# A new order of PE, ACT and DVE within the eight cycles of a batch of the first layer

## The reference

```
x = x + attn(layernorm(x))
  dist   = arccosh(1 + 2*|q-k|^2 / ((1-|q|^2)*(1-|k|^2)))
  out    = softmax(-dist) @ v ; out @ wo.T
x = x + moe(layernorm(x))
  logits = x @ router_w.T ; the 8 largest of 64 probabilities, normalised
  routed = sum over the 8 experts of weight * expert(x), at most 128 tokens each
  shared = (silu(x @ gate) * (x @ up)) @ ws_down
```

## Time and profile before

| | us |
|---|---|
| median of 3 runs (3197.37 to 3205.93) | 3198.28 |
| profiled execution, its own time | 3206.46 |
| its span | 3204.7 |
| PE, DVE, ACT, POOL busy | 2482.1, 2018.2, 1689.0, 1891.3 |
| mean granted clock of PE over the span | 0.84 |

### The profile page before, as it was taken

The page is one execution under the profiler, slowest core; times in us unless marked ns, Lnnn a source line. Parts: engine busy times, 40 slices in busy tenths (PEclk is TensorE's granted clock), DMA queues, the critical chain, the costliest instruction groups (busy, mean ns, idle before and its releaser), DMA issues. The chain is left out here.

```text
span 3204.7 us, 31378 instructions
## 1 busy us (share of the span) xinstructions
PE 2482.1 (77%) x10153; PEld 1156.9 (36%) x10153; DVE 2018.2 (63%) x3045; ACT 1689.0 (53%) x2384; POOL 1891.3 (59%) x1886
## 2 busy tenths in 40 slices
PE   4567677676766677665398699999999999999995
PEld 2222233232322222223155344444444444444442
DVE  4797868687887868672133366575656565656564
ACT  1677767767777677882022254544444444444351
POOL 0544566666756666784577304683847565655675
PEclk7667777777777787776699799999999999999996
DMA  2000000000000100002499600000000000000000
GB/s 93 14 1 1 15 14 14 15 14 15 7 9 14 15 14 7 16 9 27 113 280 263 148 1 1 1 1 20 1 20 1 21 1 14 7 7 1 7 1 14
DMA packets 95157, 99.12 MB, mean 31 GB/s; under 512 B 19825, under 2 KB 91761, under 8 KB 94961
## 3 DMA queue, kind: packets, MB, share of 16 engines
q1 hardware_dynamic: 70784, 74.12, 8.2%
q0 software_dynamic: 24176, 22.70, 3.9%
HBM read 74.30 MB, written 26.80 MB: 32 GB/s over the span
## 5 line engine op out<-in xcount | busy, mean ns | idle before, releaser
L849 POOL TENSOR_TENSOR TT<-TT,SS 128x512 f32<-128x512 f32 x512 | 651.7, 1307 | 407.9 <-ACT SS L780 407.6
L1540 ACT ACTIVATE PR<-S,NM 128x512 f32<-128x512 f32 x512 | 347.0, 683 | 579.9 <-DVE NM L1707 579.9
L1707 DVE TENSOR_REDUCE NM<-S 128x2 f32<-128x1024 f32 x256 | 313.1, 1223 | 289.1 <-PE S L1444 288.8
L372 PE MATMUL OB<-TT,VAL 128*17 128x512 f32 x1024 | 350.9, 790 | 87.0 <-ACT TT L788 86.8
L613 DVE TENSOR_SCALAR TT<-SC 128x1024 f32<-128x1024 f32 x256 | 311.5, 1217 | 132.9 <-PE SC L351 61.9
L854 POOL DMA_INDIRECT slot_tokens<-TID,IDX x256 | 258.1, 1008 | 116.4 <-issue 86.3
L615 DVE SCALAR_TENSOR_TENSOR SS<-SC,TT 128x1024 f32<-128x1024 f32 x256 | 313.6, 1225 | 20.6 <-issue 1.8
L1444 PE MATMUL S<-KT,QT 64*128 64x512 f32 x1024 | 308.2, 670 | 0.7 <-ACT QT L1509 0.7
L1473 PE MATMUL OT<-PT,VN 128*64 128x512 f32 x1024 | 284.6, 635 | 2.9 <-ACT PT L1546 2.1
L1455 PEld LDWEIGHTS TP<-ident,PR 128*128 128x128 f32 x2048 | 227.4, 141 | 147.2 <-issue 119.5
L1455 PE MATMUL TP<-ident,PR 128*128 128x128 f32 x2048 | 275.4, 278 | 5.4 <-DVE PT L1712 4.9
(11 more groups left out here) (258 smaller groups left out, 4317.4 us busy)
## 6 DMA issues: line engine op xcount, KB each, us to landing
WG<-w_gu SPq DMA_DIRECT2D x64, 384.0 KB
WD<-w_dn SPq DMA_DIRECT2D x64, 128.0 KB
stream<-rows SPq DMA_DIRECT2D x1, 4224.0 KB, 17.1
XL<-x SPq DMA_DIRECT2D x8, 512.0 KB, 4.3
X<-x SPq DMA_DIRECT2D x8, 512.0 KB, 4.0
rows<-XL SPq DMA_DIRECT2D x8, 512.0 KB
slot_tokens<-TID,IDX POOLq DMA_INDIRECT x256
stream<-X SPq DMA_DIRECT2D x8, 512.0 KB
```

The lines of the kernel that those rows point to most:

```text
L372: ins = pe.matmul(OB[r:r + DH0 + 1, :], values_of[:, mt, h, :], TT[:, h % RING, mt, :], start=(mt == 0), stop=(mt == NT - 1))
L849: ins = pool.tensor_tensor(tt[:, mt, :], tt[:, mt, :], ss[:, mt, :], ALU.add)
L1540: act.activation(PR[s % 2][h2][:], S[s % 2][:, h2, :], ACT.Exp, bias=NM[:, s % 2, h2:h2 + 1], accum_out=SM[:, pair % 2, j, h2:h2 + 1]).the ...
L1707: dve.tensor_reduce(NM[:, s % 2, :], S[s % 2][:], AX, ALU.max, negate=True).then_inc(sems["peak"], 1)
```

## The change

The lists are ordered anew, and three things move in the engines' own order:

- ACT: the first root stands ahead of slot 0. Slot 1 moves from between the roots to behind the second root and the table load, slot 2 from there to behind the first logarithm (with slot 3). `Silu` stays behind the second root.
- PE: the first score quarter of the next pair comes behind slot 3; the second comes behind the late tasks and slot 5, directly ahead of `query_norms`; slot 6 comes last.
- Tasks: `logits` from cycle 5 to 6, `weights` ahead of `slots`, `shared` 0 from cycle 1 to 0, `output` 1 and `stats2` from cycle 3 to 4, `turn_hid` 0 from cycle 0 to the end of the cycle 7 before it. Evictions go from slots 4 to 6 to others.

Numbers and kinds of operations stay as they are; one wait for `took_a` is added ahead of the first `gate_up`.

```diff
 TO_ACT = [
-    (0, 1, "turn_hid", 0, "before2"), (0, 2, "turn_hid", 1, "before2"),
-    (0, 4, "refill", 12, "this"), (0, 5, "refill", 13, "this"), (0, 6, "refill", 14, "this"), (1, 0, "refill", 15, "this"),
-    (1, 1, "turn", 0, "after"), (1, 2, "turn", 1, "after"),
-    (1, 4, "project", 0, "after"), (1, 5, "project", 1, "after"), (1, 6, "project", 2, "after"), (2, 0, "project", 3, "after"),
-    (3, 1, "turn_ao", 0, "before"), (3, 2, "turn_ao", 1, "before"),
-    (5, 0, "refill", 0, "after"), (5, 1, "turn2", 0, "before"), (5, 2, "turn2", 1, "before"),
-    (5, 3, "refill", 1, "after"), (5, 4, "refill", 2, "after"), (5, 5, "refill", 3, "after"),
-    (6, 0, "refill", 4, "after"), (6, 1, "refill", 5, "after"), (6, 3, "refill", 6, "after"), (6, 4, "refill", 7, "after"),
-    (7, 0, "refill", 8, "after"), (7, 1, "refill", 9, "after"), (7, 3, "refill", 10, "after"), (7, 4, "refill", 11, "after"),
+    (0, 1, "refill", 12, "this"), (0, 3, "turn_hid", 1, "before2"), (0, 6, "refill", 13, "this"),
+    (1, 0, "refill", 14, "this"), (1, 1, "turn", 0, "after"), (1, 2, "refill", 15, "this"),
+    (1, 2, "turn", 1, "after"), (1, 5, "project", 0, "after"), (1, 6, "project", 1, "after"),
+    (2, 0, "project", 2, "after"), (2, 1, "project", 3, "after"), (3, 0, "turn_ao", 0, "before"),
+    (3, 3, "turn_ao", 1, "before"), (5, 0, "refill", 0, "after"), (5, 0, "refill", 1, "after"),
+    (5, 0, "turn2", 0, "before"), (5, 1, "refill", 2, "after"), (5, 2, "turn2", 1, "before"),
+    (5, 5, "refill", 3, "after"), (6, 1, "refill", 4, "after"), (6, 2, "refill", 5, "after"),
+    (6, 3, "refill", 6, "after"), (6, 4, "refill", 7, "after"), (7, 1, "refill", 8, "after"),
+    (7, 3, "refill", 9, "after"), (7, 4, "refill", 10, "after"), (7, 4, "refill", 11, "after"),
+    (7, 5, "turn_hid", 0, "before"),
 ]
 TO_DVE = [
-    (0, "late", "stats", 0, "after"), (0, "late", "take_group", 2, "before"), (0, "late", "place_group", 2, "before"),
-    (0, "late", "norm", 0, "after"),
-    (1, "early", "shared", 0, "before2"), (1, "early", "shared", 1, "before2"),
-    (2, "late", "take_group", 3, "before"), (2, "late", "place_group", 3, "before"), (2, "late", "values", 0, "after"),
-    (2, "late", "norms", 0, "after"), (2, "late", "values", 1, "after"), (2, "late", "clamp_sign", 0, "after"),
-    (3, "early", "clamp_apply", 0, "after"), (3, "late", "output", 0, "before"), (3, "late", "output", 1, "before"),
-    (3, "late", "stats2", 0, "before"),
-    (4, "late", "take_group", 0, "this"), (4, "late", "split", 0, "after"), (4, "late", "split", 1, "after"),
-    (4, "late", "place_group", 0, "this"), (4, "late", "norm2", 0, "before"),
-    (5, "late", "split", 2, "after"), (5, "late", "logits", 0, "before"), (5, "late", "gate_up", 0, "before"),
-    (5, "late", "gate_up", 1, "before"), (5, "late", "split", 3, "after"),
-    (6, "early", "gate_up", 2, "before"), (6, "early", "gate_up", 3, "before"), (6, "late", "take_group", 1, "this"),
-    (6, "late", "split", 4, "after"), (6, "late", "split", 5, "after"), (6, "late", "place_group", 1, "this"),
-    (7, "early", "slots", 0, "before"), (7, "late", "split", 6, "after"), (7, "late", "split", 7, "after"),
-    (7, "late", "weights", 0, "before"),
+    (0, "early", "take_group", 2, "before"), (0, "late", "stats", 0, "after"), (0, "late", "shared", 0, "before2"),
+    (0, "late", "place_group", 2, "before"), (0, "late", "norm", 0, "after"), (1, "early", "shared", 1, "before2"),
+    (2, "late", "take_group", 3, "before"), (2, "late", "values", 0, "after"), (2, "late", "norms", 0, "after"),
+    (2, "late", "values", 1, "after"), (2, "late", "place_group", 3, "before"), (2, "late", "clamp_sign", 0, "after"),
+    (3, "early", "clamp_apply", 0, "after"), (3, "late", "output", 0, "before"), (4, "early", "output", 1, "before"),
+    (4, "early", "stats2", 0, "before"), (4, "late", "take_group", 0, "this"), (4, "late", "split", 0, "after"),
+    (4, "late", "place_group", 0, "this"), (4, "late", "norm2", 0, "before"), (4, "late", "split", 1, "after"),
+    (5, "early", "split", 2, "after"), (5, "late", "gate_up", 0, "before"), (5, "late", "gate_up", 1, "before"),
+    (5, "late", "split", 3, "after"), (6, "early", "logits", 0, "before"), (6, "early", "split", 4, "after"),
+    (6, "early", "take_group", 1, "this"), (6, "late", "gate_up", 2, "before"), (6, "late", "gate_up", 3, "before"),
+    (6, "late", "split", 5, "after"), (6, "late", "place_group", 1, "this"), (7, "early", "weights", 0, "before"),
+    (7, "early", "slots", 0, "before"), (7, "early", "split", 6, "after"), (7, "early", "split", 7, "after"),
 ]
...
             def gate_up(v, j, par):
+                if j == 0:
+                    turned_in(v)
                 product(item_d(v), j, wgu, 2 * F).then_inc(sems["work_d"], 1)
...
                 attend(v, par, p, 3, **of)
+                a_slot(v, a_parts, par, p, 3, **of)
                 if follows:
                     scores(v, ahead, 0)
-                a_slot(v, a_parts, par, p, 3, **of)
-                if follows:
-                    scores(v, ahead, 1)
                 a_slot(v, a_parts, par, p, 4, **of)
                 d_tasks(v, d_parts, par, p, ("late",), **of)
                 a_slot(v, a_parts, par, p, 5, **of)
-                a_slot(v, a_parts, par, p, 6, **of)
+                if follows:
+                    scores(v, ahead, 1)
                 if follows:
                     query_norms(v, ahead)
+                a_slot(v, a_parts, par, p, 6, **of)
...
+                if roots:
+                    root(v, h_root)
                 a_slot(v, parts, par, p, 0, **of)
                 if roots:
-                    root(v, h_root)
-                a_slot(v, parts, par, p, 1, **of)
-                if roots:
                     root(v, h_root + 1)
-                a_slot(v, parts, par, p, 2, **of)
                 if p == 7 and of["before"]:
                     act.wait_ge(sems["gu"], v.next("gu"))
                     act.activation(GU[:, :, 0:F], GU[:, :, 0:F], ACT.Silu).then_inc(sems["silu"], 1)
                 if numerators:
                     act.preload_act_table_set("natural_log_exp_and_others")
+                a_slot(v, parts, par, p, 1, **of)
+                if numerators:
                     logarithm(v, h_num)
+                a_slot(v, parts, par, p, 2, **of)
                 a_slot(v, parts, par, p, 3, **of)
```

## The result

The changed kernel's median is 3021.98 us (4 runs, 3020.83 to 3025.34), against 3198.43 for the kernel before beside it: a ratio of 0.9451, with a 95% interval of 0.9434 to 0.9469. That is 176 us, or 5.5%, less.

A forecast was written before the change was run, and what follows sets the result against it. The prediction took the order of work among four in-order queues as the bound, no engine being full. Its terms gave 18.5 us a batch, with the other batches 117.5, so 3198.3 became 3080, range 3025 to 3165.

The forecast's parts named there:

- Term 1: Cycles 0 to 2: roots ahead of slot 0 and moved refills let ACT start earlier; 8 us a batch, bounds 3 and 11.
- Term 2: Cycle 3: second head's adds end about as DVE starts `clamp_apply`; 2.5 us a batch less, bounds 0 and 2.7.
- Term 3: Cycle 7: earlier roots and `weights` first spare `slots` the adds; 3.5 us a batch less, bounds 5 less and 2 more.
- Term 4: Cycles 5 and 6: `gate_up` sooner, `logits` early in cycle 6; 4.5 us a batch less, bounds 0 and 9.
- rival A: Whole kernel: PE stays at the high clock level and adds miss every locked task; 154 us gained, 3044; chance 0.15.
- Term 5: Cycles 0 and 4, moved score quarter: no change; bound 1 us more in each of five cycles.
- slack for cycle 4: Cycle 3: ACT's gain of about 5 us is no gain of DVE, only slack for the next cycle.
- The other batches: Batches outside 2 to 6: gains of 8 us in batch 0, 12 in batch 1, 5 in batch 7.
- The signs forecast for it: On DVE: L706 near 0.42, L567 below 8 a batch, first-quarter waits about 10; ACT's cycle 1 within 2 us of DVE's.
- the terms' upper bounds: Whole kernel: every term at its largest gain, 27.7 us a batch, 176 in all, giving 3022.
- C: Whole kernel: adds move along with DVE's tasks, so overlap only shifts; 43 us gained, 3155; chance 0.25.
- D: Cycles 0, 2, 4, 5, 6: second score quarter comes late, making the kernel slower, 3218 to 3256; chance 0.10.

The follow-up runs named there:

- e8: The changed kernel with `slots` ahead of `weights` again in cycle 7, as before the change: 3025.07 us.
- e1: The kernel before with only ACT's new order, lists and PE's order left old: 3064.23 us, ratio 0.960.
- e5: The changed kernel with PE's old order (second score quarter again behind slot 3, slot 6 ahead of `query_norms`): 3022.94 us.
- e3: The kernel before with only the new lists and the added wait ahead of `gate_up`, engines' orders left old: 3152.49 us.
- e11: The kernel before with only ACT's first root moved ahead of slot 0: 3210.69 us, ratio 1.004.
- e7: The kernel before with ACT's new order alone, and L513 of `norms` written as a two-input operation: 3064.58 us.
- e9: The kernel before with each of POOL's adds cut to 64 of its 512 columns: 3139.29 us, ratio 0.9815.
- e10: The changed kernel with each of POOL's adds cut to 64 of its 512 columns: 2963.37 us, ratio 0.9265.

## Why the prediction was wrong in size and right in kind

**The bound** was named rightly. No engine is full after either (DVE 652.4 of 762.5 us, 86%), and the gain came from order alone: 128 us from a few lines of ACT's queue.

**Term 1, cycles 0 to 2** (forecast 8): cycles 1 and 2 lost 9.6, of which 0.7 is `shared` 0, moved to cycle 0. So 8.9. ACT's cycle 1 begins 0.55 us behind DVE's in batch 6 (989.49 above), where about 1 was laid out:

```profile
990.04 1.28 ACT L780 ACT_TABLE_LOAD   x1
```

**Term 2, cycle 3** (2.5): it lost 5.9; 2.8 of that are `output` 1 and `stats2`, moved to cycle 4, and the clamp's operations take 2.6 less from first to last (7.67 to 5.03 in batch 6). So 3.1.

**Term 3, cycle 7** (3.5): it lost 4.4. `slots` no longer meets the adds, `weights` does. But e8 shows that the exchange as such is worth nothing that can be measured, since `slots` first gives the same time. ACT's order alone takes 2.9 off this cycle, the lists alone 3.3. The sentence on `weights` in the prediction counts four operations with two inputs in SBUF; the kernel has three (L736, L742, L745).

**Term 4, cycles 5 and 6** (4.5, bounds 0 and 9): they lost 7.8. **This is the step that failed inside a batch.** The layout gave 17 to 21 and 21 to 26.6 us, and 19 and 22.7 were taken; measured were 16.4 and 20.9, just below the lower end of both. (The bounds 0 and 9 don't follow from that layout either: it spans 1.4 lost to 8.2 gained.) All that the term names as gain is the lists' doing: `logits` a cycle later, `gate_up` sooner. Measured alone, the lists bring 2.0 there. ACT's order alone, with the old lists, brings 5.7 (e1). So what was left out is what the roots ahead of the evictions give in these two cycles.

A second reason lies in how long PE's products take, which the layout had between two values. PE's timeline of the kernel after, in the place of the earlier trace rows:

```profile
1006.76 1.96 PE L306 MATMUL WKA<-wqkv,XT 128*128 128x512 f32 x4 [1.08 <-ACT QK L796]
...
1009.62 1.98 PE L306 MATMUL WKA<-wqkv,XT 128*128 128x512 f32 x4
```

Behind a wait of 1.08 us this projection takes 1.96, not 3.75. The sentence that gave rival A only 0.15 was that the slow projection comes right behind a wait for ACT and such waits stay. In cycle 5 `logits` and two products of `gate_up` took 3.68 and 4.84 in the kernel before; in the kernel after the two `gate_up` take 2.85 there, and `logits` 2.00 in cycle 6:

```profile
1235.77 3.68 PE L308 MATMUL WKD<-wrt,XT 128*128 128x64 f32 x16 [1.30 <-ACT QT L801]
1239.24 4.84 PE L308 MATMUL WKD<-wgu,XT 128*128 128x384 f32 x8
```

```profile
1075.70 2.85 PE L306 MATMUL WKD<-wgu,XT 128*128 128x384 f32 x8
...
1086.31 2.00 PE L306 MATMUL WKD<-wrt,XT 128*128 128x64 f32 x16
```

The granted clock was 0.50 during the 3.75 and the 3.68, 0.58 during the 4.84, and 1.00 during each of the short ones. By cycles of the same batch of after it is 1.00 in cycle 1, 0.90 in cycle 2, 0.74 in cycle 5 and 0.89 in cycle 6; over five batches it rose only from 0.75 to 0.78. So these products ran at the 2.4 GHz level while the mean stayed a mix. PE's groups for `gate_up`, batches 2 to 6 of e1 and then of after, show how far that carries:

```profile
L308 PE MATMUL WKD<-wgu,XT 128*128 128x384 f32 x80 | 35.8, 602 | 0.0
```

```profile
L306 PE MATMUL WKD<-wgu,XT 128*128 128x384 f32 x80 | 28.0, 493 | 0.0
```

In e1 they are about as slow as before (614 ns each), and cycles 5 and 6 are 5.7 shorter all the same, so the faster `gate_up` can't be the larger part of term 4. How much of the 176 us is the clock's wasn't measured apart from the shorter waits: no run held it still.

**Term 5, cycles 0 and 4** (0, bound 5 lost): 2.1 us less when the moved work is put back (cycle 0 became 0.7 shorter though 0.7 of work moved in; cycle 4 became 2.1 longer though 2.8 moved in). The moved score quarter cost nothing (e5). That the "slack for cycle 4" of the forecast was worth something fits this, and e1's cycle 4 (15.3 against 16.8), but isn't shown.

**The other batches** (25 forecast: 8, 12, 5): 18.8, 20.4 and 4.9, together 44.1. **This is the step that failed outside them.** Batch 0 was scaled down because it has no routing and batch 1 because it has no shared expert. But ACT's roots, logarithms, turns and refills run in both. Batch 1 gains mostly by ACT's order (16.2 us in e1, 3.2 in e3), batch 0 by both (6.9 and 10.7). This miss (19.1) is a little larger than term 4's in all five batches (3.3 x 5 = 16.5). With 38.5 more in batches 2 to 6 and 6 outside the cycles they make up the 63.6 by which the profiled execution beat the sum.

**The lock's price.** The signs forecast for it came true (L706 0.43, casts 5.5 a batch against "below 8", waits of a quarter 10.4 against "about 10"; ACT's cycle 1 starts 0.6 to 0.8 behind DVE's, against "within 2"); a batch of "about 160" didn't (152.5). Terms 2 and 3 counted a us of lock as a us of batch. That holds nearly in the new order (7.5 for 6.8) and not in the old one (18.1 for 8.0), and the forecast had no way to tell the two apart. Signs that come true don't prove the price that was put on them.

**The rivals.** A's time (154 a batch, 3044) was nearest; its high clock is seen in part (0.78 over five batches), its "adds miss every locked task" isn't (`weights` meets them). C fell, as L706 and the batch show. D fell: in batches 1 to 7 of after no second quarter waits for PE at all, and in batch 0 one does, 1.15 us. Once the terms' upper bounds gave 3022, the range's low end of 3025 was too high; it should have gone past them, for term 5 was bounded at no gain, and batches 0 and 1 with the rest at 38, where 50 came. That the measured time equals the 3022 of the upper bounds is luck: the batches gave less than their bound (26.2 for 27.7), the rest more.

## What to carry to other kernels

Where engines hand work over through one bank, put an in-order engine's long operations, on which others wait, ahead of evictions that may not be ready: evictions ahead of the second root and the first logarithm cost more here (67 us) than all the lists together (40). Try both halves of such an order together as well as apart: one half alone (e11) made the kernel slower, and nearly a third of what ACT's order gained in a batch (5.7 of 18.3 us) came only with both. Before pricing time lost to a shared port as time of the kernel, take the other engine's work away once, in the order that you mean to keep: here it was worth less than half in the old order and nearly all in the new one.

## What the runs showed of the hardware beyond that

**An operation of DVE can be shut out for a whole run of POOL's instructions.** L513 took 9.44 us beside eight adds (e1) and 4.49 beside four (e11, in every batch from 2 to 6), ending with the last add; mostly an operation that meets the adds takes 1.33, about one add (1303 ns). The kernels before and after have it too, beside eight adds: in before two casts (L567, at 1032.83) take 6.60 us, where such a pair usually takes 0.5 to 1.3, and in after the operation below, 4 elements wide and usually 0.17 long, takes 5.33:

```profile
904.92 5.33 DVE L482 TENSOR_SCALAR var<-mv 128x4 f32<-128x4 f32 x1
```

Runs of eight adds that shut DVE out took 9.78 to 9.86 us; the run of eight that `slots` got in between the earlier trace rows took 10.71. The Trainium skill (SBUF — State Buffer, "Who interferes with whom") has it that whoever issues first gets the shared pair for the whole instruction and the other is blocked until it ends. The rows of 1.33 agree; 9.44 and 4.49 are longer than one instruction and don't. One or two SBUF inputs isn't what separates them (e7), and what does stays open.

**A gap ahead of a scatter.** Once within the cycles POOL stands 8 to 9 us ahead of a scatter with nothing that the trace shows to wait for. The rows are of before and of after:

```profile
1025.66 0.96 POOL L854 DMA_INDIRECT slot_tokens<-TID,IDX  x1 [8.92 <-issue]
```

```profile
896.87 0.97 POOL L855 DMA_INDIRECT slot_tokens<-TID,IDX  x1 [8.84 <-issue]
```

It comes ahead of the 114th of the 256 scatters, and again ahead of the 227th, in all fourteen profiles here, wherever they lie in time; so it goes by the count. Its cause is open. In itself it costs nothing here: with the adds cut to an eighth the gap is there (8.20 in e9, 8.49 in e10), and cycle 4 of that batch is as long as in the others (14.8 and 17.8). In the kernel after cycle 4 of that batch lasts 22.9 us instead of 17.9, because the delayed adds come as a run of eight (900.38 to 910.23) and shut L482 out, 5.33 instead of 0.17; in before it is the cast, and 21.0 instead of 15.8. As both kernels have it, it explains nothing of the difference between them.
